# Weight-scratch stores issued from GpSimd instead of SyncE, and one scaling moved from GpSimd to VectorE, in a recurrent layer with gated feed-forward on eight cores

## What is computed

```python
xn = layernorm(x)
# recurrent branch
gate, xa = split(xn @ w_in.T)                   # 2048 output features
xc = causal_conv4(xa) + b_conv
forget, inp = split(xc @ w_gates.T + b_gates)   # 2048 output features
alpha = exp(-8 * softplus(forget_base) * sigmoid(forget))
beta  = sqrt(1 - alpha**2 + 1e-6)
u = beta * sigmoid(inp) * xc
h = scan(h = alpha * h + u)                     # along time
s = (gelu(gate) * h) @ w_out.T                  # 1024 output features
# feed-forward branch: pick one of 8 components per feature
logits = (xn @ sel_w.T + sel_b).reshape(b, s, 1024, 8)
comp   = xn @ comp_w.T + comp_b                 # 8 x 1024 features
g = silu(comp[argmax(logits)])
out = x + s * g
```

## Time and profile before

| What | us |
|---|---|
| median of 2 runs | 4389.8 |
| the two runs | 4264.6 and 4515.0 |
| the profiled execution, its own time | 3993.52 |
| its span on the slowest core (core 7) | 3992.0 |
| spans of all cores | 3970.4 to 3992.0 |
| granted TensorE clock, mean of a core | 0.965 to 0.970 |
| busy: PE, DVE, ACT, POOL | 3624.2, 1240.9, 619.1, 442.7 |

### The profile page before, as it was taken

The page is one execution under the profiler, slowest core; times in us unless marked ns, Lnnn a source line. Parts: engine busy times, 40 slices in busy tenths (PEclk is TensorE's granted clock), DMA queues, the critical chain, the costliest instruction groups (busy, mean ns, idle before and its releaser), DMA issues.

```text
span 3992.0 us, 42537 instructions; the slowest of 8 cores (3970.4 to 3992.0 us)
## 1 busy us (share of the span) xinstructions
PE 3624.2 (91%) x16272; PEld 1600.6 (40%) x16272; DVE 1240.9 (31%) x1696; ACT 619.1 (16%) x819; POOL 442.7 (11%) x280
## 2 busy tenths in 40 slices
PE   1887888887688899999999899999999899999997
PEld 0333333333233344444444344444444344444443
DVE  1413222332125342233224342223224342223223
ACT  1243122112121140000010140000010140000000
POOL 2233333333332010000000010000000000000000
PEclk8998999999889999999999999999999999999998
DMA  3345544444434343333323332222222423323232
GB/s 96 116 147 150 157 151 166 156 158 150 156 114 148 120 127 99 102 106 99 102 87 103 128 118 104 106 102 100 106 85 98 132 98 106 103 98 106 96 105 95
DMA packets 197496, 468.44 MB, mean 117 GB/s; under 512 B 14992, under 2 KB 101024, under 8 KB 197296
## 3 DMA queue, kind: packets, MB, share of 16 engines
q1 hardware_dynamic: 194688, 457.24, 34.8%
q0 software_dynamic: 2608, 8.49, 0.8%
HBM read 369.20 MB, written 96.47 MB: 117 GB/s over the span
## 4 chain that ended last, share of the span: by engine, by line
PE 62%; DMA 15%; POOL 8%; DVE 6%; ACT 4%; issue 2%; SPq 2%; DVEq 0%; ACTq 0%; POOLq 0%
PE pg L301 61%; POOL wl L87 7%; DMA w<-cmpT 5%; DMA w<-selT 4%; ACT wh L87 2%; DVE poolC L87 2%; SPq L271 1%; DVE poolB L87 1%; DMA w<-w2T 1%; DMA w<-w1T 1%; DMA poolA<-xT 1%; DMA outT<-poolC 1%; PE pg L371 1%; PE pg L365 1%; DVE accb L87 1%
## 5 line engine op out<-in xcount | busy, mean ns | idle before, releaser
L301 PE MATMUL pg<-xnh,wh 128*128 128x512 bf16 x4608 | 1767.0, 383 | 217.9 <-POOL wl L87 152.0
L301 PE MATMUL pg<-xnl,wh 128*128 128x512 bf16 x4608 | 1766.7, 383 | 0.0
L301 PE MATMUL pg<-xnh,wl 128*128 128x512 bf16 x4608 | 1765.6, 383 | 0.0
L301 PEld LDWEIGHTS pg<-xnh,wh 128*128 128x128 bf16 x4608 | 454.8, 99 | 801.3 <-issue 275.8
L87 DVE TENSOR_SCALAR si<-pg,vecsb 128x512 f32<-128x512 f32 x256 | 192.2, 751 | 1843.9 <-PE pg L301 1843.9
L301 PEld LDWEIGHTS pg<-xnh,wl 128*128 128x128 bf16 x4608 | 455.1, 99 | 557.0 <-issue 23.4
L301 PEld LDWEIGHTS pg<-xnl,wh 128*128 128x128 bf16 x4608 | 454.6, 99 | 547.4 <-issue 21.2
L87 POOL TENSOR_TENSOR wl<-w,wh 128x1024 bf16<-128x1024 f32 x168 | 363.4, 2163 | 807.3 <-ACT wh L87 795.7
L87 ACT ACTIVATE sf<-pg 128x512 f32<-128x512 f32 x256 | 152.8, 597 | 1615.1 <-DVE msk L87 936.6
L301 PE MATMUL pg<-xch,wh 128*128 128x512 bf16 x768 | 295.3, 385 | 29.2 <-POOL wl L87 28.3
L87 ACT ACTIVATE wh<-w 128x1024 bf16<-128x1024 f32 x168 | 177.5, 1057 | 818.2 <-DMA w<-selT 289.8
(11 more groups left out here) (56 smaller groups left out, 865.9 us busy)
## 6 DMA issues: line engine op xcount, KB each, us to landing
wh<-wscr SPq DMA_DIRECT2D x252, 512.0 KB, 5.2
wl<-wscr SPq DMA_DIRECT2D x252, 512.0 KB, 6.1
wscr<-wh SPq DMA_DIRECT2D x84, 512.0 KB, 2.7
wscr<-wl SPq DMA_DIRECT2D x84, 512.0 KB, 4.8
w<-selT SPq DMA_DIRECT2D x64, 512.0 KB, 6.7
w<-cmpT SPq DMA_DIRECT2D x64, 512.0 KB, 7.0
w<-w1T SPq DMA_DIRECT2D x16, 512.0 KB, 8.4
hb<-xT POOLq DMA_DIRECT2D x32, 256.0 KB, 6.0
```

The costliest lines, as they stand in the source:

```text
L301: last = tensor.matmul(bank[:, :], wop[:, wcol:wcol + P], xop[:, k * TT:(k + 1) * TT], start=(idx == 0), stop=(idx == 23))
```

## The change

Two things. The stores of wh and wl to `wscr` are issued from POOL's queue instead of SP's; the explicit wait of SP for the last subtraction goes, since POOL's own order (and its wrapper's wait) gives it. The scaling of scr in `emit_EL_a` runs on DVE instead of POOL, and ACT's logarithm waits for DVE's semaphore.

```diff
@@ pump_split
                 for pc, buf in ((0, wh), (1, wl)):
-                    c.needt(sync, "sync", lo_toks[-1])
-                    ins = sync.dma_start(
+                    ins = gpsimd.dma_start(
                         out=wscr[hs * P:(hs + 1) * P, pc * 2048:(pc + 1) * 2048],
                         in_=buf[par][:, :])
                     c.inc(ins, gwn, 16)
@@ emit_EL_a
-                    c.need(gpsimd, "gp", "sc", c.cnt["sc"])
-                    ins = gpsimd.tensor_scalar(SC, SC, -1.0, 1.0 + 1e-6,
+                    c.need(vector, "ve", "sc", c.cnt["sc"])
+                    ins = vector.tensor_scalar(SC, SC, -1.0, 1.0 + 1e-6,
                                                OP.mult, OP.add)
-                    ztok = ("gpc", c.inc(ins, "gpc"))
+                    ztok = ("ve", c.inc(ins, "ve"))
```

## The result

The changed kernel takes 3731.6 us (median of 13 runs), the kernel before 3995.5 (median of 10). The ratio is 0.935, with a 95% interval of 0.9339 to 0.9361: 6.5% faster. The profiled execution took 3729.0 us, and its span on core 6 is 3727.5. Both medians take in slow runs, in which, as far as clocks are on record here, the cores of one die have a lower granted clock (0.84 to 0.95 where the others have 0.985); the ratio leaves them out, and the two times of before that were shown ahead of the prediction (4264.6 and 4515.0) are among them.

The account below looks back on a forecast made before the run. TensorE was the busiest engine, held up in tile 0 by a serial load-split-store loop on SP. Savings of 261 + 4 + 0 + 0 = 265 us gave 3728 us (-6.7%), scaled to 4098 on the median; range 3700 to 4300.

Parts of the forecast that it names:

- The scale: Whole time: the gap of 396 us between median and profiled execution scales with everything, giving 4098 us instead of 3728.
- The loop on SP: Tile 0: with stores off SP two loads overlap, 6.7 us per half instead of 14.24, so TensorE sets the pace.
- The term of 180.3 + 61.3 us: Tile 0: 180.3 us of PE's waits for wl and 61.3 us of lower clock go, together 241.6 us.
- The wait for the squares: Tile 0, before the next LayerNorm: PE's wait falls from 30.4 to 8.8 us, freeing 22 us.
- The wait for xnl: Tile 0: PE's wait for xnl stays at 7.6 us.
- The start: Before tile 0: POOL issues the xT loads one split earlier; gain 4 us, between a loss of 3 and gain of 11.
- The stores on POOL: Weight halves: two more DMA issues each on POOL, 0.53 us apiece; price 0, at worst 2 us.
- The scaling on DVE: Block pairs: ACT's second logarithm comes 1.9 us later per pair; price 0, bound 8 us in tile 0.
- Transfers as the bound: Rival, tile 0: slower DMA transfers set the pace, saving falls to about 80 us, time 4300; chance 0.06.
- Lower clock in tile 0: Rival: tile 0's granted clock stays under full even without waits; time 4257, -3.0%; chance 0.14.
- POOL blocked: Rival: store issues block POOL, at 6 us each a half takes 17 us; 227 us lost, +5.7%; chance 0.04.
- No effect: Rival: loads still wait behind their predecessor's split, the loop stays at 14 us, time 4390; chance 0.04.

Follow-up runs that it names:

- e1: The changed kernel with the scaling of scr back on POOL, so only the stores are moved; ratio 0.9346 to the kernel before.
- e4: The kernel before, stores still on SP but issued behind the next float32 load, scaling still on POOL; ratio 0.9342.
- e3: The changed kernel, stores on POOL, but SP waits for the split's last subtraction before issuing the next float32 load; ratio 0.9853.
- e5b: The changed kernel with each of a half's two stores cut into eight, so 16 store issues per half on POOL; 4034.1 us, one execution.
- e2: The kernel before with only the scaling of scr moved to DVE; ratio 1.0073.
- e2b: The kernel before with only the scaling of scr moved to DVE, the edit of e2 measured again in more rounds; ratio 1.0008.

## Why the prediction was right and where it was wrong

**The scale: wrong.** "If the gap scales everything, the answer is 4389.8 x 0.933 = 4098 us, which I take." This is the step that failed. The sum made against the profiled execution gave 3728; measured are 3729.0 for the profiled execution and 3731.6 for the median. The kernel before measures 3995.5, so 4098 would have been slower than it. The step took the 396 us between the two times shown and the profiled execution for time that the kernel needs and that the change only scales. But six of the ten times of before lie between 3983.2 and 3996.1, and the profiled execution (3993.5) is like them. The two times shown came without a profile and without clocks. Where times of that height have clocks on record, these are low: 4522.3 us with 0.82 to 0.85 on the eight cores, against 0.967 to 0.971 at 3993.4 (both of the kernel before, measured with e1 to e4). I carried the result over to the pair whose cause I could not see, and so threw a good sum away. The forecast of -6.7% stands against -6.5%. That the 3728 came within a microsecond of the profiled execution is in part luck, since tile 0 lost 245 us on one core and 263 on another.

**The loop on SP: right.** Two loads in flight and TensorE's pace was the claim; the period is 10.36 us and the waits for wl are zero. The pace was taken at 10.6 us. The term of 180.3 + 61.3 us came back whole: no wait, clock 0.99, and TensorE's busy time in tile 0 fell from 949.8 to 886.9 us (889.8 in e4, whose trace has 80 more of the matmul records). e3 and e4 show that it is the order on the queue, in both directions.

**The wait for the squares: right.** 8.8 us were worked out, 7.8 measured. The wait for xnl was kept at 7.6 and is 6.4. Tile 0: 907 predicted, 905.5 measured.

**The start: the number right, by luck.** 4 us were taken as the middle of a wide range, from a loss of 3 to a gain of 11; 3.6 measured. The xT loads were issued 4.5 us earlier (at 36.9 us and not 41.4), but they took no shorter time: from issue to the first square 17.7 us, where it was 17.0. Nor does one pair of cores settle 4 us: tile 0 starts at 112.5 to 116.7 us on the eight cores before and at 108.3 to 113.1 after, and in e1, with the same order at the start, at 115.4 on the slowest core.

**The stores on POOL: right that they cost nothing.** 0.53 us an issue was taken, 0.56 and 0.55 measured, half of the upper bound; e5b shows what it costs once POOL's sum passes TensorE's pace. The Trainium skill ("SBUF — State Buffer", section "SBUF: two separate sides") warned of POOL-issued DMAs. Their landing is later indeed, 7.0 and 8.6 us where SP's took 2.7 and 4.8, also in e3 (7.1 and 8.4), where tile 0 is otherwise slow again. In e4, with equal traffic but stores on SP, they land in 2.7 and 4.8. So the path costs some 4 us a store. VectorE's lock, which the page names, isn't the main part of it here: the stores of the changed kernel's tile 0 during which DVE did nothing at all (12 of wh, 9 of wl) landed in 7.0 and 8.0 us, those with over 2 us of DVE work beside them (45 and 46) in 7.0 and 8.8. What else of that path costs the 4 us stays open. As foreseen, nobody waits for it.

**The scaling on DVE: right.** ACT's logarithm of the second block was to be 1.9 us later; its wait grew from 1.45 us to 3.16 in tile 1 (timelines of DVE and ACT after the change):

```profile
1140.01 0.43 DVE L87 TENSOR_SCALAR scr<-scr 128x512 f32<-128x512 f32 x1
...
1140.59 0.63 ACT L87 ACTIVATE scr<-scr 128x512 f32<-128x512 f32 x1 [3.16 <-DVE scr L87]
```

That is 1.7 us. In the changed kernel none of it reaches the end, as e1 shows. In the kernel before, whose loop has no slack, some 5 us of it show in tile 0 (e2, e2b); the bound of 8 us was the better number there than the 0.

**The rivals.** Transfers as the bound: no, the DMA share came out at 0.61 as worked out, and loads land in 7.2 us (6.7 before). Lower clock in tile 0: no, 0.99. POOL blocked: no, but e5b shows it can be had. No effect: no, the loads no longer stand behind the split of their predecessor.

## What to carry to other kernels

A queue that issues both a load and a store that waits for the work on the previous load is a serial loop, whatever number of buffers stands behind it. Look at the period of such a loop in the timeline, compare it with the bound engine's pace, and put the load ahead of the waiting store; a change of order on the same queue does as much as a second queue. When two numbers of the kernel before disagree and only one has a profile, predict against that one, as the cause of the other can't be seen.

## What the runs showed that I had not expected

DVE slowed down in tile 0 without new work of note. It is busy 395.9 us instead of 345.0, of which the 8 scalings are some 4; in e1, which has none of them, 390.9, and in e4, with stores on SP, 382.3. In e3, with the same instructions as the changed kernel but spread over 1097 us, DVE is back at 348.5.

The trace shows what holds DVE: POOL's subtractions. Two rows of the changed kernel (timelines of POOL and DVE at 364 us):

```profile
363.06 2.13 POOL L87 TENSOR_TENSOR wl<-w,wh 128x1024 bf16<-128x1024 f32 x1 [1.41 <-ACT wh L87]
363.17 2.56 DVE L87 SCALAR_TENSOR_TENSOR mxb<-sf,vecsb,mxb 128x512 f32<-128x512 f32 x1
```

The maximum takes 0.75 us in the median. Here it starts 0.11 us into the subtraction and ends at 365.73, 0.54 after the subtraction's end. In tile 0 of the changed kernel 65 DVE instructions are over 0.2 us longer than the median of their kind (counted from the starts and lengths in the trace), and 63 of them start while a subtraction runs; each of these ends 0.28 to 0.59 us after it. The two others start during a store issue and end 0.56 us after the subtraction that follows; the longest maximum, 3.1 us, is one of them. The 31 instructions that start in a subtraction and read PSUM, the memory that the matmuls write (such as si<-pg), keep their length. Before, 38 instructions were caught in this way and lengthened by 60 us in all; in e3 it is 39 and 61, in e4 59 and 100, in the changed kernel 63 and 106. So DVE pays when its work falls beside the subtractions more often, as it does when the same work is packed into a shorter tile.

The Trainium skill, "SBUF — State Buffer", section "SBUF: two separate sides", says that a VectorE instruction with two SBUF inputs and a GpSimd instruction that reads SBUF exclude each other. The trace agrees: the 50 held instructions with two inputs or more (maxima, masks, products, predicated copies) end 0.54 to 0.59 us after the subtraction. It shows 13 more with one input each (casts, copies, scalings) held as well, ending 0.28 us after it; the sentence on two inputs doesn't cover these.

Packing is not all: in e5b tile 0 takes 1188.3 us and DVE is busy 420.0 in it. Most instructions that start during a store issue keep their length there (263 of 288), but the 25 others, held over the subtraction that comes next or up to its start, are 73 us longer together. TensorE did not wait for DVE longer for any of it in the changed kernel (6.4 us at the end of tile 0, 7.6 before).

Stores issued from POOL land 3.8 to 4.3 us later than the same stores from SP, at equal traffic (the changed kernel against e4).
